# Gated FFN plus linear attention on one core: the last full step gets programs of its own on TensorE and VectorE, and the last pair is summed on VectorE and stored in halves

## The reference

```
xn = layernorm(x)
# attention branch, per batch of 2048 rows
Q, K, V = xn @ Wq.T + bq, xn @ Wk.T + bk, xn @ Wv.T + bv
Q, K = each column divided by its norm over the 2048 rows
matrix = K applied to V                                # 256 x 256 per batch
s = xn + gamma * (sum(V) + Q @ matrix) * tailor        # tailor = 1 / (256 + Q . (sum(K) + eps))
# feed-forward branch; fq = blockwise FP4 quantise and dequantise, blocks of 16
h = silu(fq(xn) @ fq(w_gate).T) * (fq(xn) @ fq(w_up).T)     # I = 704 wide
g = silu(fq(h) @ fq(w_down).T)
out = x + s * g
```

## Time and profile before

| | |
|---|---|
| median of 3 runs | 618.38 us (617.84 to 620.1) |
| the profiled execution's own time | 619.48 us |
| its span, first to last instruction | 617.7 us, mean granted TensorE clock 0.983 |
| TensorE busy | 553.6 us (90%), 4957 matmuls |
| VectorE busy | 565.4 us (92%) |
| ScalarE busy | 410.7 us (66%) |
| POOL busy | 245.8 us (40%) |

### The profile page before, as it was taken

How to read it: one execution, slowest core, us unless ns; L and a number is a source line. 1 busy time by engine, 2 the same in 40 slices (tenths; PEclk the granted TensorE clock), 3 DMA queues, 4 the chain that set the end, 5 groups by cost and what they waited for, 6 DMA issues and landing times. The chain is left out here.

```text
span 617.7 us, 15155 instructions
## 1 busy us (share of the span) xinstructions
PE 553.6 (90%) x4957; PEld 428.2 (69%) x4957; DVE 565.4 (92%) x1195; ACT 410.7 (66%) x884; POOL 245.8 (40%) x208
## 2 busy tenths in 40 slices
PE   0366879999999999989999989989999999999886
PEld 0243567777787777758887766758888777778775
DVE  6979899999999999989999997999999999987873
ACT  3565768877787786757776766747677777644431
POOL 4443233433343334434243343452353454422146
PEclk9998899999999999989999998989999999999999
DMA  7000001000001101110111111011111110013133
GB/s 242 17 35 18 18 2 24 18 30 8 12 19 35 36 18 53 52 54 2 53 53 53 54 54 56 12 41 53 54 53 53 53 37 23 30 41 132 35 120 137
DMA packets 17473, 29.15 MB, mean 47 GB/s; under 512 B 2672, under 2 KB 4848, under 8 KB 17392
## 3 DMA queue, kind: packets, MB, share of 16 engines
q1 hardware_dynamic: 17392, 28.13, 13.8%
HBM read 19.73 MB, written 8.39 MB: 46 GB/s over the span
## 5 line engine op out<-in xcount | busy, mean ns | idle before, releaser
L1350 PE MATMUL GU<-wgu,xqT 128*128 128x352 f16 x1536 | 259.0, 320 | 6.1 <-DVE h L855 3.4
L1350 PEld LDWEIGHTS GU<-wgu,xqT 128*128 128x128 f16 x1536 | 150.6, 100 | 84.6 <-issue 7.1
L602 ACT ACTIVATE sil<-GU,wkap 128x352 f32<-128x352 f32 x128 | 70.7, 553 | 74.7 <-PE GU L1350 73.7
L521 POOL TENSOR_TENSOR ht<-h,hrr 128x1408 f32<-128x1408 f32 x32 | 82.8, 2588 | 85.6 <-DVE hrr L869 84.1
L1360 PE MATMUL DS<-wdT,hqT 128*128 128x256 f16 x704 | 87.3, 272 | 1.9 <-ACT hqT L609 1.9
L855 DVE SCALAR_TENSOR_TENSOR h<-GU,wkap,sil 128x352 f32<-128x352 f32 x128 | 69.3, 542 | 18.1 <-ACT sil L602 17.8
L903 DVE TENSOR_TENSOR hq<-hg,hs 128x704 f16<-128x704 f16 x128 | 78.3, 653 | 0.9
L487 POOL TENSOR_TENSOR xnat<-xs,xnat 128x510 f16<-128x510 f32 (+1 forms) x32 | 37.0, 1157 | 100.5 <-DVE hq L903 96.8
L477 POOL TENSOR_TENSOR rs<-ve,half 128x2 f32<-128x2 f32 x32 | 25.2, 787 | 126.8 <-DVE ht L892 112.8
L1360 PEld LDWEIGHTS DS<-wdT,hqT 128*128 128x128 f16 x704 | 66.8, 98 | 11.9 <-ACT hqT L609 2.3
L638 ACT ACTIVATE gring<-DS,hun 128x256 f32<-128x256 f32 (+1 forms) x64 | 29.8, 466 | 43.8 <-issue 29.6
(11 more groups left out here) (156 smaller groups left out, 955.1 us busy)
## 6 DMA issues: line engine op xcount, KB each, us to landing
xin<-in_L_attn_x SPq DMA_DIRECT2D x34, 256.0 KB, 2.8
xe<-in_L_attn_x SPq DMA_DIRECT2D x25, 256.0 KB, 2.8
out<-o SPq DMA_DIRECT2D x25, 256.0 KB, 2.1
algebra<-in_L_ffn_w_down SPq DMA_DIRECT2D x1, 704.0 KB, 6.6
gring<-in_L_ffn_w_gate SPq DMA_DIRECT2D x1, 640.0 KB, 4.5
gring<-in_L_ffn_w_up SPq DMA_DIRECT2D x1, 640.0 KB, 5.3
xs<-in_L_attn_x SPq DMA_DIRECT2D x2, 256.0 KB, 4.5
xt<-in_L_attn_x SPq DMA_DIRECT2D x2, 256.0 KB, 5.0
```

What stands on the lines that cost most here:

```text
L521: g.tensor_tensor(paired(ht[:, 0:2 * I]), paired(h[:, q]), spread(hrr[:, q], 4 * CB), ALU.mult).then_inc(S["ht_d"], 1)
L602: a.activation(sil[:, c], GU[:, c, 0, 0:CH], ACT.Silu, scale=wkap[:, 0:1]).then_inc(S["sil_d"], 1)
L1350: last = t.matmul(GU[:, c, m, 0:CH], xqT[:, k, j, 2 * a_ + kc], wgu[:, b_, kc, 2 * m + c], start=(z == 0 and kc == 0), stop=(z == 2 and kc ...
```

## The change

Nothing before step p = 32 is changed. `drive` ends one step earlier for the engines that have a tail (TensorE, VectorE, ScalarE), and their tails begin with that step.

- **TensorE, step 32.** The down product of tile 60 moves ahead of "top", the S product of tile 44 and the transposes of tile 61 between "top" and "high_low", the S products of tiles 45, 46 and 47 behind "high_low", and the down product of tile 61 behind those.
- **TensorE, tail.** The S products of pairs 24 and 25 stand together, then the transposes of both tiles of pair 31, the S products of pair 26, both down products with nothing between them, and the S products of pairs 27 to 31.
- **VectorE.** `e_half` moves ahead of the answer "top"; `e_mul` of tiles 44 and 45 stand behind "high_low"; `e_mul` of tile 46 stands between `ht` and `hg`, that of tile 47 between `hg` and the four `hq`. The other `e_mul` follow.
- **The last pair.** `e_mul` of tiles 62 and 63 writes into G, a PSUM bank that is no longer needed; VectorE, not POOL, adds x, a tile at a time (`o_last`), and SP stores each half (128 KB, rows of 1 KB) on its own. POOL's last sum goes away.
- **ScalarE.** The same instructions in the same order.

```diff
@@ -267,11 +267,9 @@
 
         ASKS_END = {(-2, 1, 2): "gram0_0", (-1, 0, 1): "gram0_1", (-1, 1, 1): "gram0_2", (0, 0, 0): "gram0_3",
                     (0, 1, 0): "gram1_0", (0, 1, 1): "gram1_1", (1, 0, 0): "turn", (1, 0, 2): "t1q",
-                    (1, 1, 1): "t1k", (2, 0, 0): "norms", (2, 0, 2): "raw", (2, 1, 1): "tailor", (3, 0, 0): "product",
-                    (3, 0, 1): "top", (3, 0, 3): "high_low"}
+                    (1, 1, 1): "t1k", (2, 0, 0): "norms", (2, 0, 2): "raw", (2, 1, 1): "tailor"}
         ANSWERS_END = {(0, 0, 2): "gram0", (0, 1, 2): "gram1", (1, 0, 1): "turn", (1, 1, 2): "squares",
-                       (2, 0, 1): "norms", (2, 1, 2): "tailor", (2, 1, 3): "scale", (3, 0, 0): "product",
-                       (3, 0, 1): "top", (3, 0, 4): "high_low"}
+                       (2, 0, 1): "norms", (2, 1, 2): "tailor", (2, 1, 3): "scale"}
         COPIES_END = {(1, 1, 0): "t1q", (2, 1, 0): "raw"}
 
         def at_step(table, table_end, b, at):
@@ -299,7 +297,7 @@
                 for i in range(4, PB + 4):
                     later, step = batch_step(i)
                     iteration(b * PB + i, i % 2, b + later, step)
-            for p in range((BATCHES - 1) * PB + 4, PAIRS + 1):
+            for p in range((BATCHES - 1) * PB + 4, PAIRS if tail else PAIRS + 1):
                 iteration(p, p % 2, *batch_step(p))
 
             if tail:
@@ -433,8 +431,15 @@
                         sp.dma_start(xend[z], rows(xf, PAIRS - ENDS + z)).then_inc(S["xend_in"], 16)
                 if on["o"]:
                     e = p - LAGO
-                    wait(sp, "o_d", e + 1)
+                    if not (isinstance(e, int) and e == PAIRS - 1):
+                        wait(sp, "o_d", e + 1)
                     ko = (k + LAGO) % 2
+                    if isinstance(e, int) and e == PAIRS - 1:
+                        for j in range(2):
+                            own = slice(j * D, (j + 1) * D)
+                            sp.wait_ge(S["last_d"], j + 1)
+                            sp.dma_start(rows(of, e)[:, own], end_row(p)[:, own]).then_inc(S[f"out_d{ko}"], 16)
+                        return
                     sp.dma_start(rows(of, e), end_row(p) if at_end(p) else o[:, ko]).then_inc(S[f"out_d{ko}"], 16)
                 if on["e"] and not (isinstance(p, int) and p - LAGE >= PAIRS - ENDS):
 
@@ -443,7 +448,7 @@
 
             drive(sp, iteration)
             sp.wait_ge(S["out_d0"], 8 * PAIRS + 16)
-            sp.wait_ge(S["out_d1"], 8 * PAIRS + 16)
+            sp.wait_ge(S["out_d1"], 8 * PAIRS + 16 + 16)
 
 
         @block.gpsimd
@@ -524,7 +529,7 @@
                 if i == 3 and not last_batch:
                     wait(pool, "nrm_d", b + 1)
                     g.tensor_tensor(inv[:, :], nrm[:, :], half[:, :], ALU.pow).then_inc(S["inv_d"], 1)
-                if on["o"]:
+                if on["o"] and not (isinstance(p, int) and p - LAGO == PAIRS - 1):
                     e, ko = p - LAGO, (k + LAGO) % 2
                     wait(pool, "y_d", 4 * e + 4)
                     if at_end(p):
@@ -784,6 +789,7 @@
                     g_out(p, k, 1, on["e"])
 
             def tail():
+                iteration(PAIRS, PAIRS % 2, *batch_step(PAIRS))
                 p = PAIRS + 1
                 for j in range(2):
                     hidden_out(p, j)
@@ -915,6 +921,16 @@
                                        s_spare(0, 1 - c) if last else s_spare(c), unm[:, 0:1],
                                        ring(gring, e, GRING)[:, row, c * P:(c + 1) * P], ALU.mult, ALU.mult).then_inc(S["y_d"], 1)
 
+            def y_last(j):
+
+                return G[:, j * D:(j + 1) * D]
+
+            def o_last(j):
+                own = slice(j * D, (j + 1) * D)
+                dve.wait_ge(S["xend_in"], 16 * ENDS)
+                dve.wait_ge(S["y_d"], 4 * PAIRS - 2 + 2 * j)
+                v.tensor_tensor(xend[ENDS - 1][:, own], y_last(j), xend[ENDS - 1][:, own], ALU.add).then_inc(S["last_d"], 1)
+
             def e_mul(p, k, j):
                 e = p - LAGE
                 n = 2 * e + j
@@ -923,7 +939,8 @@
                 if j == 0:
 
                     wait(dve, "o_d", e - 1)
-                v.scalar_tensor_tensor(y[:, (k + LAGE) % 2, j * D:(j + 1) * D], GU[:, j, k, 0:D], unm[:, int(e >= PAIRS - PB):int(e >= PAIRS - PB) + 1],
+                to = y_last(j) if e == PAIRS - 1 else y[:, (k + LAGE) % 2, j * D:(j + 1) * D]
+                v.scalar_tensor_tensor(to, GU[:, j, k, 0:D], unm[:, int(e >= PAIRS - PB):int(e >= PAIRS - PB) + 1],
                                        ring(gring, e, GRING)[:, j], ALU.mult, ALU.mult).then_inc(S["y_d"], 2)
 
             def answer(b, step):
@@ -1226,9 +1243,28 @@
                     h_scales(p, k, 2)
 
             def tail():
-                for p in range(PAIRS + 1, PAIRS + LAGE):
+                p, k, b = PAIRS, PAIRS % 2, BATCHES - 1
+                e_half(p, k, 0, 0)
+                answer(b, "product")
+                parts(p, k, 0)
+                parts(p, k, 1)
+                e_half(p, k, 0, 1)
+                answer(b, "top")
+                answer(b, "high_low")
+                e_mul(p, k, 0)
+                e_mul(p, k, 1)
+                parts(p, k, 2)
+                h_round(p, k, 0)
+                e_mul(p + 1, 1 - k, 0)
+                h_round(p, k, 1)
+                e_mul(p + 1, 1 - k, 1)
+                h_round(p, k, 2)
+                h_round(p, k, 3)
+                for p in range(PAIRS + 2, PAIRS + LAGE):
                     for j in range(2):
                         e_mul(p, p % 2, j)
+                        if p == PAIRS + LAGE - 1:
+                            o_last(j)
 
             drive(dve, iteration, tail)
 
@@ -1538,18 +1574,32 @@
                     for j in range(2):
                         s_product(p, p % 2, j, last, e == PAIRS - PB and j == 0)
 
-                p, k, first = PAIRS + 1, (PAIRS + 1) % 2, PAIRS + 1 - LAGE
+                p, k = PAIRS, PAIRS % 2
+                s_half(p, k, 0, 0, last, PB - 5)
+                for c in range(2):
+                    hidden_transposes(p, k, 0, c, False)
+                ask(last, "product")
+                s_half(p, k, 0, 1, last, PB - 5)
+                down_product(p, k, 0)
+                ask(last, "top")
+                s_product(p, k, 0, last, False)
+                for c in range(2):
+                    hidden_transposes(p, k, 1, c, False)
+                ask(last, "high_low")
+                s_product(p, k, 1, last, False)
+                s_pair(PAIRS + 1 - LAGE)
+                down_product(p, k, 1)
+
+                p, k, first = PAIRS + 1, (PAIRS + 1) % 2, PAIRS + 2 - LAGE
                 s_pair(first)
                 s_pair(first + 1)
-                for c in range(2):
-                    hidden_transposes(p, k, 0, c, False)
+                for j in range(2):
+                    for c in range(2):
+                        hidden_transposes(p, k, j, c, False)
                 s_pair(first + 2)
-                for c in range(2):
-                    hidden_transposes(p, k, 1, c, False)
                 down_product(p, k, 0)
-                s_pair(first + 3)
                 down_product(p, k, 1)
-                for e in range(first + 4, PAIRS):
+                for e in range(first + 3, PAIRS):
                     s_pair(e)
 
             drive(pe, iteration, tail)
```

More of the change, by code:

```diff
@@ L210, in build @@
             nrm_d inv_d n_tr n_ev raw_mm raw_ev cs_mm cs_ev pm_mm den1 gi_d
-            tmp_d mt_d mtop_d top_mm kap1 kap_d unm_d m_tr mhi_d mats""".split()
+            tmp_d mt_d mtop_d last_d top_mm kap1 kap_d unm_d m_tr mhi_d mats""".split()
         S = {n: sem(n) for n in names}
```

## The result

| | before | changed |
|---|---|---|
| median | 618.23 us (617.84 to 620.1, 4 runs) | 625.88 us (624.36 to 626.76, 4 runs) |
| profiled execution, own time | 619.48 us | 625.81 us |
| its span, mean granted clock | 617.7 us, 0.983 | 624.0 us, 0.973 |
| ratio, 95% interval | | 1.0109 [1.0087, 1.0131] |

The changed kernel is **1.1% slower**: 6.7 us by the ratio, 7.7 us between the two medians of four runs. The forecast was 621.1 us with a range to 622.9, so the sign of its lean was right and the size was far off. The two profiled executions differ by 6.3 us of span, and those can be placed one by one.

The account below looks back on a forecast made before the run. TensorE's last run of S products was taken to set the end. The terms +1.5 + 1.3 - 0.8 + 0.7 = +2.7 us gave 622.2 us against the profiled execution, 621.1 us against the median; range 617.9 to 622.9 us.

Parts of the forecast that it names:

- What bounds the kernel: Last 30 us: TensorE's last ten S products set the end; whatever delays them delays the end.
- Parts 1 and 2: Step 32: 3.4 us of TensorE's waits filled, but with VectorE's hq later only 0.45 us is left.
- the meeting: POOL's sums and VectorE's ht, hg and hq wait for one another over shared SBUF access, predicted at 2.0 us.
- Part 3: POOL's sums of pairs 22 and 23 delay hg and hq 2.0 us; transposes of tile 62 start 1.5 us later.
- Part 4: Transposes of tile 62 to last S products: pair 26's S products move out of a wait that stays, cost 1.3 us.
- Part 5: Last pair: last issue 0.55 us earlier and 0.25 us from the smaller store, gain 0.8 us.
- Part 6: TensorE's clock: one fall likely from 595.3 to 601.5 us, 0.7 us taken, bounds 0 and 1.7.
- a rival with a chance of 0.18: Clock also falls after the wait between the last down products, adding 1.7 us: 4.4 us slower, 622.8 us; chance 0.18.
- the signs listed beforehand: Included hg at 2.4 us, one hq at 1.6, 2.1 us idle before the last down product, last S products from 609.3.

Follow-up runs that it names:

- experiment 2: Changed kernel with POOL's sums from pair 22 on held until the last hq is written: 619.01 us, ratio 0.9994 to the kernel before.
- Experiment 7: experiment 6 with S products of pairs 25 and 26, high_low and e_mul reordered to follow operand arrival: 615.89 us, ratio 0.9936 to the kernel before.
- experiment 6: Changed kernel with POOL held until the last hq and ScalarE's pair 31 copies ahead of g_out: 618.37 us, ratio 0.9978 to the kernel before.
- experiment 1: Changed kernel with unread matmuls filling TensorE's waits in its tail: 622.01 us, ratio 1.0033 to the kernel before.
- experiment 3: Changed kernel with ScalarE's copies of pair 31 ahead of its two g_out: 621.9 us, ratio 1.0032 to the kernel before.
- experiment 9: Changed kernel with 15 unread matmuls only between the last two down products: 624.45 us, ratio 1.0066 to the kernel before.
- experiment 10: Experiment 7 without the wait that holds POOL back: 617.07 us, ratio 0.9955 to the kernel before.
- experiment 11: Experiment 7 with 14 unread matmuls per batch in a main loop wait of TensorE: 614.99 us, ratio 0.9921 to the kernel before.

## Why the prediction was wrong where it was

- **What bounds the kernel: right.** TensorE's last run of S products sets the end, and every microsecond before it arrived there.
- **Parts 1 and 2: right, a little pessimistic.** The down product of tile 60 starts 0.34 us behind the S half, and the 3.4 us of filled waits vanish at `hq`. The last write of Mx_end comes 1.45 us later than before, 0.36 of them from upstream (predicted: 1.2). Without the meeting the transposes of tile 62 would start 0.90 us earlier than before, where I had 0.45 (599.15 - 0.36 - 1.73 against 597.96).
- **Part 3: right.** 1.73 us for the meeting, predicted 2.0; experiment 2 gives 1.76. Of the four `hq`, one takes 1.58 us and the others 0.51, and `hg` 2.30 us, close to the 1.6 and 2.4 that were to show it. The rule that I had set against the change, GPSIMD Engine Reference, section Specifications, in the Trainium skill, is borne out. The split was different: x of pair 22 landed earlier, so POOL's first sum was held by `ht` for over a microsecond, then held `hg` for 0.68 instead of 0.8, and the `hq` lost 1.05 instead of 1.2. Both parts together: +0.83 at the transposes, predicted +1.5.
- **Part 4: right.** 1.31 us moved out of a wait that stays at 1.94 us (predicted 2.1); experiment 2, with no fall of the clock, has 1.37. Experiment 7 shows the other side: put back between the down products, the same S products cost 0.45 us there instead of 1.37 (against experiment 6, where the wait had already been shortened).
- **Part 5: half right.** 0.59 and 0.54 us instead of 0.8. The last issue begins 0.45 us earlier, predicted 0.55: SP takes 0.43 to 0.45 us to issue a half, not the 0.3 of a whole block, so the second half waits for the first. Of the 0.25 us for half the data some 0.1 is there at most, since both sizes land in 2.0 us.
- **Part 6, TensorE's clock: this is the step that failed.** I took 0.7 us for "one such fall, over work that partly waits anyway", with 1.7 as the bound; measured, 4.4 us in the timeline and 4.7, give or take 1.6, by experiment 1. Two things were wrong in it. The first fall lasted 6.8 us, not the 3.4 that rows 11 show ((0.08 + 0.34) x 4 / 0.5), and the work in it is all on the path: the second transposes, two S products and most of a down product, 1.77 + 0.95 = 2.7 us. And the second fall, which I had as a rival with a chance of 0.18, came in both profiled executions of the changed kernel, at the place the rival named and for the price it named (1.34 + 0.33 = 1.67, named 1.7). The rival was the right mechanism, and 2.0 us too cheap for the first fall. Of the signs listed beforehand it is the last ten S products that show it: they start at 613.07 us, not at 609.3.

The sum with the measured terms: 0.36 upstream, +0.83, +1.31, -0.59 and +4.4 make 6.3 us, the difference of the spans. Had only Part 6 been right, the forecast would have been 2.0 + 4.4 = 6.4 us, 624.8 us, "slower".

The argument against the second fall was a stretch of step 32 that had been busy for 1.69 of 3 us and kept its clock. Experiments 2 and 3 point to what it left out. The same 1.94 us wait brings no fall when the stretch before it ran at full clock (experiment 2); behind the 6.8 us of low clock it does, twice out of two; and with that low stretch but a shorter or a filled wait it doesn't (experiments 3 and 9). I priced the two falls as independent events, and in these profiles they hang together. That rests on one profile of each of experiments 2, 3 and 9; it is not shown whether the low stretch itself matters, or only how waits and work lie in time, or which kind of work stands between them (transposes or products). What the rule behind this is stays open: the clock fell with no wait over 1.94 us in the changed kernel and did not fall with one of 2.49 us in experiment 10, so the length of a single wait is not the measure. The Trainium skill, TensorE: Matmul & The Clock Gate, section Why this matters for your kernels, asks for no long idle gap between bursts; none of the gaps in this tail was longer than 1.94 us, and the clock fell twice, so looking only at single gaps would not have warned.

So the change went wrong at three places that hold together. Filling TensorE's waits in step 32 released POOL into VectorE's long instructions (1.7 us). The same reordering left two waits with nothing in them (1.3 us). And the waits gathered close together, so the clock fell, twice (4.4 us). That is 7.4 us, and 0.4 lie upstream of the change; against it stand 0.9 us that step 32 would have gained and 0.6 of the last pair, which leaves the 6.3 of the spans. Without the clock, 6.3 - 4.4 = 1.9 us remain; experiment 1 measures 0.0033 or 2.0 us.

## What to carry to other kernels

When work of the bounding engine is moved, look at where its waits then stand in relation to each other: several waits of 1.15 to 1.94 us with little work between them cost 4.4 us here by the clock, on top of their own length, so work belongs into each of them rather than behind all. If there is no useful work to put there, matmuls into a free bank held the clock up here (experiments 1, 9 and 11), and in the tail, where they fit the waits, every dependent step kept its distance (experiment 1). An engine that had been idle at the right time by accident, POOL here, may have to be kept idle by a wait once its input comes earlier.

## What I had not expected of the hardware

- The falls of TensorE's clock in the kernel before behind 250 us last 3.3 to 3.4 us each; the first fall in the changed kernel's tail lasts twice that, 6.8 us of the lower level, in both its profiles and in those of experiments 3 and 9.
- TensorE waited for 2.49 us in one piece at full clock in experiment 10, and the clock stayed at 1.00; in the loop of the kernel before it fell behind a wait of 2.56 us.
- POOL and VectorE hold each other for the rest of the whole instruction: 2.59 us for a POOL sum of 1.25, 2.58 us for an `hg` of 1.62. Beside POOL's last sums VectorE's instructions with one operand in PSUM stay at 0.42 and 0.48 us.
- A store of 128 KB in rows of 1 KB lands in the same 2.0 us as one of 256 KB in rows of 2 KB.
